# Score chunks of the first head inside the last context tiles, and an output projection in three parts

## The reference

```
x = x + cross_attention(layernorm(x), ctx)   # ctx: 4096 x 512
x = x + state_space(layernorm(x))
x = x + experts(layernorm(x))

cross_attention: q, k, v of x (16 heads, 4 kv heads of 128), k and v of ctx;
  q, k, k_ctx with a root-mean-square norm per head, q and k also rotated;
  keys = 4096 of ctx and 256 own ones (causal); softmax; @ wo
state_space: z, xBC, dt = u @ W_in; causal convolution of 4 taps and silu on xBC;
  dt = softplus(dt + bias); two chunks of 128 tokens: decays exp(cs_l - cs_s) under
  the diagonal, y = (C B^T * decays) (x dt) + C state + D x; y = y * silu(z);
  y = y * rsqrt(mean(y*y) + eps) * norm_weight; @ W_out
experts: top 6 of 32 experts (192 wide) by sigmoid scores, and a shared one (384 wide)
```

## Time and profile before

| | |
|---|---|
| time of the runs (3) | median 1052.37 us, 1051.82 to 1052.49 |
| the profiled execution | 1051.38 us |
| its span, first to last instruction | 1049.3 us |
| TensorE busy | 1035.7 us (99%) |
| VectorE busy | 777.2 us (74%) |
| ScalarE busy | 602.7 us (57%) |
| GpSimd busy | 182.4 us (17%) |
| granted TensorE clock | 1.00 over the whole span |

### The profile page before, as it was taken

The page is one execution under the profiler, slowest core; times in us unless marked ns, Lnnn a source line. Parts: engine busy times, 40 slices in busy tenths (PEclk is TensorE's granted clock), DMA queues, the critical chain, the costliest instruction groups (busy, mean ns, idle before and its releaser), DMA issues.

```text
span 1049.3 us, 15552 instructions
## 1 busy us (share of the span) xinstructions
PE 1035.7 (99%) x5789; PEld 885.7 (84%) x5789; DVE 777.2 (74%) x1661; ACT 602.7 (57%) x1090; POOL 182.4 (17%) x200
## 2 busy tenths in 40 slices
PE   7999999999999999999999999999999999999998
PEld 6888888887888888888888888888886888888887
DVE  5856777648777777777877777877668877777775
ACT  4344434334865566665566666568448466666664
POOL 4643344330000000000000000002202112222221
PEclk9999999999999999999999999999999999999999
DMA  6658675498004240042200431004450376555540
GB/s 235 233 195 286 229 241 173 133 317 293 37 1 139 73 131 1 1 171 81 91 1 1 171 121 56 1 1 182 161 231 1 121 285 214 195 191 183 190 169 21
DMA packets 64155, 145.76 MB, mean 139 GB/s; under 512 B 3888, under 2 KB 42704, under 8 KB 62672
## 3 DMA queue, kind: packets, MB, share of 16 engines
q1 hardware_dynamic: 64080, 144.77, 40.0%
HBM read 108.55 MB, written 36.21 MB: 138 GB/s over the span
## 4 chain that ended last, share of the span: by engine, by line
PE 95%; DVE 2%; ACT 1%; POOL 0%; issue 0%; DMA 0%; ACTq 0%
PE bank L549 18%; PE bank L486 16%; PE bank L592 12%; PE bank L569 11%; PE bank L467 11%; PE bank L847 8%; PE bank L594 6%; PE bank L849 4%; PE bank L649 2%; PE bank L662 1%; PE bank L496 1%; PE bank L780 1%; PE bank L717 1%; DVE e_hl L1192 0%; PE bank L818 0%; PE bank L521 0%
## 5 line engine op out<-in xcount | busy, mean ns | idle before, releaser
L1058 DVE TENSOR_TENSOR pT<-bank,pT 128x512 fp32r<-128x512 f32 x272 | 184.8, 689 | 103.3 <-ACT pT L1485 101.5
L1485 ACT CAST pT<-bank 128x512 fp32r<-128x512 f32 x272 | 156.1, 594 | 142.7 <-PE bank L569 139.5
L592 PE MATMUL bank<-pT,vN 128*128 128x512 f32 (+1 forms) x544 | 225.7, 422 | 0.0
L549 PE MATMUL bank<-kT,qT_hi 128*128 128x512 f32 (+2 forms) x576 | 214.5, 391 | 2.1 <-DVE scores L1002 2.1
L1002 DVE TENSOR_SCALAR_CACHE_REDUCE scores<-bank 128x512 f32<-128x512 f32 x256 | 172.8, 686 | 1.7
L569 PE MATMUL bank<-ident,scores 128*128 128x128 f32 x1072 | 161.3, 272 | 0.4 <-DVE pT L1058 0.3
L1456 ACT ACTIVATE scores<-scores,neg_max 128x1024 f32<-128x1024 f32 (+2 forms) x128 | 154.0, 1203 | 5.7 <-DVE neg_max L1014 5.7
L594 PE MATMUL bank<-pT,vN 128*128 128x256 f32 (+1 forms) x544 | 152.5, 280 | 0.0
L486 PE MATMUL bank<-w_ctx_hi,ctx_hl 128*128 128x512 f32 x512 | 146.0, 398 | 6.5 <-ACT ctx_hl L1365 6.5
L847 PE MATMUL bank<-fT_parts,e_hl 128*128 128x512 f32 x392 | 140.0, 395 | 0.1
L569 PEld LDWEIGHTS bank<-ident,scores 128*128 128x128 f32 x1072 | 127.2, 140 | 12.1 <-DVE pT L1058 1.2
(11 more groups left out here) (224 smaller groups left out, 1563.9 us busy)
## 6 DMA issues: line engine op xcount, KB each, us to landing
e_raw<-in_experts SPq DMA_DIRECT2D x51, 768.0 KB, 4.3
k_spill<-k_stage SPq DMA_DIRECT2D x16, 1024.0 KB, 4.5
v_spill<-v_stage SPq DMA_DIRECT2D x16, 1024.0 KB, 8.4
vN<-v_spill SPq DMA_DIRECT2D x16, 1024.0 KB, 5.2
kT<-k_spill SPq DMA_DIRECT2D x15, 1024.0 KB, 5.3
ctx_raw<-in_ctx SPq DMA_DIRECT2D x15, 512.0 KB, 4.3
w_raw<-in_w_qkv SPq DMA_DIRECT2D x6, 1024.0 KB, 5.0
wo_sb<-in_wo SPq DMA_DIRECT2D x4, 1024.0 KB, 9.5
```

The source lines that it names most:

```text
L549: done = e.matmul(bank[b][:, 0:n], qT[a][:, h, qt * P:(qt + 1) * P], kT[:, w, lo:lo + n], start=m == 0, stop=m == 2)
L592: e.matmul(halves[:, :, q0:L], vN[:, 0, kt, :], ring[:, :, i * L + q0:(i + 1) * L], start=kt == 0, stop=False)
L1058: e.tensor_tensor(ring[:, 1, :], bank[tb][:, :], ring[:, 0, :], ALU.subtract).then_inc(p_lo, 1)
L1485: e.copy(ring[:, 0, :], bank[tb][:, :]).then_inc(p_hi, 1)
```

## The change

**Chunks.** Nine early chunks of head 0 (all seven of qt 0, two of qt 1) are issued inside tiles 29, 30 and 31, one after each of the first three groups of `project(i)`, in banks 6 and 7 by turns; VectorE evicts them ahead of the rest of that tile. The five early chunks that are left use banks 0, 2, 6, 7, 0; three of them come ahead of `turn(NT - 1)`, two behind it. The third group starts again at bank 0. Four chunks of head 1 are made ahead, not eight. The regions v and s01 change places in the SBUF, and `chunk_max` moves to keep.

**Last tile.** ScalarE squares k of tile 31 ahead of the copy of tile 30's k. VectorE puts the low part of k of tile 30 in the place of the low part of v of tile 31, which it makes after both maxima of head 0. SP loads three pieces of v before it spills the last batch.

**Output projection.** w_out is loaded in two halves (the first with w_z, the second after wo), split by ScalarE (times norm_weight) and VectorE; y turned is split too (ScalarE copies, VectorE subtracts); `project_y` makes three products of each. Padding x waits for the first four splits. The load of expert tile 4 waits for the end of the projection.

**Decays.** For the second token tile ScalarE makes all eight heads of a half; PE's order of the decay turns and `y_rows(0, 0)` changes with it.

**Start of the experts.** The low parts of the first expert tiles are made in pieces between other steps, the first tokens are turned between the two column groups of the projection, the first logits come after the first gate products, and the second token tile's copies change places.

```diff
+EARLY = 3
-        for i, c in enumerate(EARLY_CHUNKS):
-            self.add(0, 0, c, (0, 2, 6, 7)[i % 4])
-        self.first = list(range(len(self.chunks)))
-        for c in EARLY_CHUNKS:
-            self.add(0, 1, c)
-        self.second = list(range(len(self.first), len(self.chunks)))
+        for i, (qt, c) in enumerate([(qt, c) for qt in range(2) for c in EARLY_CHUNKS]):
+            self.add(0, qt, c, (6, 7)[i % 2] if i < EARLY * 3 else (0, 2, 6, 7)[(i - EARLY * 3) % 4])
+        self.first = {NT - EARLY + i: list(range(3 * i, 3 * i + 3)) for i in range(EARLY)}
+        self.second = list(range(3 * EARLY, len(self.chunks)))
...
-        for _ in range(8):
+        for _ in range(4):
             self.ahead.append(self.add(1, *ahead.pop(0)))
...
-        sizes = dict(keep=12288, k=34816, v=34816, spare=16096, s01=34816, s23=34816, pt=12288, q=32768)
+        sizes = dict(keep=12288, k=34816, s01=34816, spare=16096, v=34816, s23=34816, pt=12288, q=32768)
...  (TensorE, project)
+                    if i in plan.first and k < KD - 1:
+                        in_turns([plan.first[i][k]], None)
...  (TensorE, after the tiles)
-            for s in plan.first:
-                in_turns([s], None)
+            in_turns(plan.second[:3], None)
             turn(NT - 1)
-            for s in plan.second + plan.third + plan.ahead:
+            for s in plan.second[3:] + plan.third + plan.ahead:
                 in_turns([s], None)
...  (TensorE, state space)
+            y_rows(0, 0, dsub_a, 1)
+            decay_rows(1, 0, 1, bnat_st, 2)
             decay_rows(1, 1, 0, xr, 6)
             decay_rows(1, 1, 1, gated_z, 4)
-            decay_rows(1, 0, 1, bnat_st, 2)
-            y_rows(0, 0, dsub_a, 1)
...  (TensorE, project_y)
+                pe.wait_ge(wo2_lo, 4 * half + 4)
...
-                        done = e.matmul(bank[b][:, 0:n], yT[:, k, tt * P:(tt + 1) * P], w_out[:, k, lo:lo + n], start=k == 0, stop=k == DI // P - 1)
+                        done = three(bank[b][:, 0:n], lambda a: yT[a][:, k, tt * P:(tt + 1) * P],
+                                     lambda w: w_out_lo[k][:, lo:lo + n] if w else w_out_hi[:, k, lo:lo + n], k == 0, k == DI // P - 1)
...  (TensorE, experts)
-            turn_rows(4, 0, fn)
-            project_y(1, 1)
-            route_logits(0)
+            project_y(1, 1, turn_between=turn_first_tokens)
...
             up_half(0, 0)
             up_half(1, 0, (0,))
+            route_logits(0)
...  (VectorE, one tile: after(i))
+                if i < NT - 1:
+                    rest_of_v(i)
+                else:
+                    rest_of_k(i - 1)
...  (VectorE, tiles)
+                if i in plan.first:
+                    for s in plan.first[i]:
+                        evict(s)
+                if 1 <= i < NT - 1:
+                    rest_of_k(i - 1)
+                after(i)
...  (VectorE, after the tiles)
+            for s in plan.second[:2]:
                 evict(s)
             rest_of_k(NT - 1)
+            for s in plan.second[2:]:
                 evict(s)
             for qt in range(2):
                 for s in plan.third[2 * qt:2 * qt + 2]:
                     evict(s)
                 maximum(0, qt)
+            rest_of_v(NT - 1)
             for s in plan.ahead:
                 evict(s)
...  (VectorE, splits)
+            def rest_of_w_out(k):
+                src = w_out_raw[k // 4][:, k % 4, :]
+                dve.wait_ge(wo2_hi, k + 1)
+                dve.wait_ge(pv, NH * NPAIR)
+                e.scalar_tensor_tensor(out=w_out_lo[k][:, :], in0=src, scalar=nw[:, k:k + 1], in1=w_out_hi[:, k, :],
+                                       op0=ALU.mult, op1=ALU.subtract).then_inc(wo2_lo, 1)
+            for k in range(4):
+                rest_of_w_out(k)
...
             mask_gram()
+            rest_of_w_out(4)
+            rest_of_w_out(5)
             mask_rows(0, 0)
+            rest_of_w_out(6)
             x_rows(1, 0)
-            decay_rows(1, 0)
+            rest_of_w_out(7)
             mask_rows(0, 1)
-            decay_rows(1, 1)
...  (ScalarE, tiles)
-                if i >= 1:
+                if 1 <= i < NT - 1:
                     main_of_k(i - 1)
-                after(i)
+                squares_of_k(i)
+                if i == NT - 1:
+                    main_of_k(i - 1)
+                main_of_v(i)
...  (ScalarE, splits and decays)
+            for k in range(6):
+                main_of_w_out(k)
...
+            def second_decay_rows(c, between=None):
+                act.wait_ge(wo2_lo, 6 + 2 * c)
+                for q in range(2):
+                    h0, b = 8 * c + 4 * q, BANK_DEC[1, c][q]
+                    act.wait_ge(drow, DROWS.index((1, c, q)) + 1)
+                    for i in range(4):
+                        done = e.activation(decays[1][:, h0 + i, :], bank[b][:, i * P:(i + 1) * P], ACT.Relu, bias=cs[:, 1, h0 + i:h0 + i + 1], scale=-1.0)
+                    done.then_inc(dsub_a, 1)
...
+                e.activation(rows, rows, ACT.Exp, scale=-1.0).then_inc(dec_e, 2)
...  (SP)
+            sp.wait_ge(ctx_proj, NT)
+            for p in (0, 1, 2):
+                wait_spilled(v_out, p)
+                load_v(0, p)
             spill(NBATCH - 1)
-            for p in (0, 1, 2, NPIECE - 1, NPIECE - 2):
+            for p in (NPIECE - 1, NPIECE - 2):
...
+            e.dma_start(w_out_raw[0][:, :, :], t["w_out"][:, 0:4]).then_inc(w_out_in[0], 16)
             sp.wait_ge(wo_done, TT)
-            e.dma_start(w_out[:, :, :], t["w_out"]).then_inc(w_out_in, 16)
+            e.dma_start(w_out_raw[1][:, :, :], t["w_out"][:, 4:8]).then_inc(w_out_in[1], 16)
...  (SP, load_e)
+                        sp.wait_ge(e_lo_first, 1)
+                    elif j == 4:
+                        sp.wait_ge(yp, 3)
```

More of the change, by code:

```diff
@@ L163, in before, with last_in @@
         return self.bank_history[bank][k - 1] if k else None
+    def last_in(self, bank):
+        return self.bank_history[bank][-1][1]
     def last_chunk(self, h):
@@ L275, in build_program @@
         pT = [reg.take(f"pT{i}", [2, 512], F32R) for i, reg in enumerate([region["pt"]] * 3 + [sp_])]
-        chunk_max = [sp_.take(f"chunk_max{i}", [NCHK]) for i in range(4)]
+        chunk_max = [keep.take(f"chunk_max{i}", [NCHK]) for i in range(4)]
         row_max = [sp_.take(f"row_max{i}", [1]) for i in range(4)]
@@ L522, in own_turn @@
                 done.then_inc(own_turned, 1)
-            for i in range(NT):
-                project(i)
-                if i == 1:
-                    pe.wait_ge(consts, 7)
-                    for tt in range(TT):
-                        pe.wait_ge(ln_out, tt + 1)
-                        turn_rows(tt, tt, xn)
-                if i >= 1:
-                    turn(i - 1)
-                n, half = step_of(i)
-                if 1 <= n <= NSTEP and half == 0:
-                    own_turn(n - 1)
-                if 0 <= n < NSTEP and half == 0:
-                    own_project(n)
             def score(s):
@@ L622, in spread_sums @@
                 done.then_inc(spread, 1)
-            for s in plan.first:
-                in_turns([s], None)
+            for i in range(NT):
+                project(i)
+                if i == 1:
+                    pe.wait_ge(consts, 7)
+                    for tt in range(TT):
+                        pe.wait_ge(ln_out, tt + 1)
+                        turn_rows(tt, tt, xn)
+                if i >= 1:
+                    turn(i - 1)
+                n, half = step_of(i)
+                if 1 <= n <= NSTEP and half == 0:
+                    own_turn(n - 1)
+                if 0 <= n < NSTEP and half == 0:
+                    own_project(n)
+            in_turns(plan.second[:3], None)
             turn(NT - 1)
-            for s in plan.second + plan.third + plan.ahead:
+            for s in plan.second[3:] + plan.third + plan.ahead:
                 in_turns([s], None)
@@ L1548, in act_program @@
             e.activation(ecs[:, :], cs[:, 1, :], ACT.Exp).then_inc(dec_exp, 1)
+            def second_decay_rows(c, between=None):
[6 more added lines that the diff above has]
+                    done.then_inc(dsub_a, 1)
+                    if q == 0 and between:
+                        between()
+                rows = decays[1][:, 8 * c:8 * c + 8, :]
+                act.wait_ge(dsub_a, 2 * c + 4)
+                e.activation(rows, rows, ACT.Exp, scale=-1.0).then_inc(dec_e, 2)
             def decay_rows(tt, c):
```

169 lines of the change are left out of this document (105 added, 64 removed).

## The result

The changed kernel takes 1055.11 us in the median of 8 runs (1054.44 to 1055.26), the kernel before 1052.32 in 8 runs beside it (1050.57 to 1052.62). The ratio is 1.0028, 95% interval 1.0019 to 1.0037: slower by 2.8 us. The profiled execution of the changed kernel took 1055.26 us with a span of 1053.4; that of before 1051.38 with 1049.3.

A forecast was written before the change was run, and what follows sets the result against it. TensorE, busy 99% of the span and 95% of the last chain, was taken to bound the kernel. Moved chunks +7.1 and output projection -2.3 gave +4.8 us on 1052.37: 1057.2 us, range 1051.5 to 1061.5.

The forecast's parts named there:

- Chunks inside the tiles cost nothing more: Tiles 29 to 31: nine moved chunks cost their own 5.83 us of TensorE work and add no waits.
- The last turn: End of the last tile: TensorE idle 1.3 us until it can turn the normalised keys at 240.27.
- The bank of the first late chunk: Late chunks of head 0: bank 0 waits for all 14 evictions, TensorE idle 2.3 us.
- The store of v and TensorE's wait: Head 0: late last v spill holds ScalarE's first pT copy, then VectorE, then TensorE, idle 5 us.
- The slow restart: Rival: after the 5 us wait twelve matmuls run at half clock, +2.4 us, 1059.6 us; chance 0.17.
- The crowded queue: Rival: the v spill meets the loads of v and k, takes 11.6 us: +4.0, 1061.2 us; chance 0.07.
- Sum of part 1: Move of nine chunks into the last three tiles, with its waits up to head 0's third step: +7.1 us.
- Part 2: Output projection in three products, with weight splits, decays and experts' start: -2.3 us, bounds -3.0 and 0.
- the wait for the first tokens: Last layer: the 0.5 us wait before the first tokens are turned goes, as they are turned between column groups.
- three places: Split of turned tokens, logits, second tokens: TensorE there before VectorE, waits of 0.1 to 0.3 us, summed as 0.35.
- From profile to median: Whole kernel: median of runs taken 0.99 us above the profiled 1051.38, giving base 1052.37 us.

The follow-up runs named there:

- the fills: Changed kernel with matmuls of no use in TensorE's two longest waits, two versions: 1053.19 us (ratio 1.0012) and 1053.28 us (1.0018).
- the three kernels of that experiment: Changed kernel with v's last low part earlier, with last spills ahead of the v loads, and with both: 1055.04, 1054.44, 1049.91 us.
- part 1 alone: Kernel before with the chunk and last-tile edits, without those of output projection, decays and experts' start: 1057.24 us, ratio 1.0052.
- the mended kernels: Kernels with the chunk and last-tile edits plus low part of v early, last spills first, late chunks from bank 1: 1048.81 us; without output-projection edits 1050.75.
- part 2 alone: Changed kernel with chunk and last-tile edits undone, output projection in three products kept: 1049.80 us, ratio 0.9981 to the kernel before.
- the mended part 1: Kernel before with chunk and last-tile edits, low part of v early, last spills first, late chunks from bank 1; no output-projection edits: 1050.75 us, ratio 0.9989.
- v early: Changed kernel with only the low part of v of the last tile earlier on VectorE: 1055.04 us, ratio 1.0033 to the kernel before.
- spills first: Changed kernel with only the last spills ahead of the three v loads on the DMA queue: 1054.44 us, ratio 1.0024 to the kernel before.
- both: Changed kernel with the low part of v earlier and the last spills ahead of the v loads: 1049.91 us, ratio 0.9983 to the kernel before.
- bank one first: Changed kernel with the late chunks beginning in bank 1 in place of bank 0: 1054.46 us, ratio 1.0027 to the kernel before.
- the shorter fills: Changed kernel with 8 and 10 matmuls of no use in TensorE's two waits, without the wait for the last keys' copy: 1053.28 us, ratio 1.0018.

## Why the prediction was right, and where its sizes were off

The forecast was slower, +4.8 us, 1057.2; measured were +2.8 and 1055.1. Direction and mechanism were right, several terms were not.

- *Chunks inside the tiles cost nothing more.* Right: the nine put the turn of tile 30 back by 5.97 us against the turn of tile 27; 5.83 was their price.
- *The last turn.* Forecast idle 1.3, measured 0.90.
- *The bank of the first late chunk.* Forecast 2.3, measured 2.17, of the same cause: it is released by the last early chunk's eviction.
- *The store of v and TensorE's wait.* The term that was most off. The idle was 5.0 in the forecast and 2.6 in the trace. Half of the difference is that TensorE itself came 1.2 us later, counted from the turn of tile 31 (260.00 - 244.87 = 15.1 in place of 13.9), delayed by its low clock: with the first wait filled it got there at 13.6 (259.95 - 246.34). The other half is the landing: TensorE goes on 17.7 us behind that turn in place of 18.9. The store was issued 1.4 us later than forecast (10.1 behind the turn for 8.8) and landed 1.3 sooner (15.7 for 16.9), so the transfer, which I had set to 8.2 us from issue, was 2.7 too long. Of these, 0.6 is a slip of reading: landings are counted from the start of the issue, and I added the 0.58 us of the issue to 7.6. The rest is the size itself, set by a least of 7.1. The landings of all sixteen stores of v in the changed kernel, and the last stores of k and v alone:

```profile
DMA to landing us min/median/max: 5.5/8.3/11.5
...
k_spill<-k_stage SPq DMA_DIRECT2D x1, 1024.0 KB, 10.8
v_spill<-v_stage SPq DMA_DIRECT2D x1, 1024.0 KB, 5.5
```

  The 5.5 is a new least. In the kernel before each store of v was issued directly behind a store of k, so its landing held that one's transfer too; here 8 us lie between the two issues (247.06 and 255.00), and the store of k, held up behind the three loads, lands at 257.8, 2.7 us ahead of that of v. The sixteen rows were a sample of another case, and their least was no bound for this one.
- *The slow restart.* It had a chance of 0.17 (though the text beside it says "about as likely as not"), "a wait of 5 us" as its condition and +2.4 us as its price. It is what happens, twice, behind waits of only 2.2 and 2.6 us; and the fills show that it costs what the second stretch loses, 1 to 2 us in the median. It should have been in the sum: that the time did not come out too low for want of it is in part luck, as the store of v landed 1.3 us sooner than forecast.
- *The crowded queue.* Its 11.6 us for the store did not come about in the changed kernel, but its mechanism did. I let the three loads pass for done since they had been issued 12 us before; the store of k that stood behind them landed 2.8 us after the store of v was issued (257.8 for 255.00). The store of v was so late that little of this delay showed in its own 5.5 us; when v was moved early the price came almost to the letter (11.4). The mistake was to see only the store of v behind the loads, and not the store of k ahead of it. The Trainium skill ("DMA: Bandwidth & Descriptors", Queues, rings and completion order) has descriptors consumed in ring order; the three kernels of that experiment agree with it (store of k: 10.9 us behind the three loads, 4.4 and 4.5 ahead of them).
- *Sum of part 1.* At the first turn of head 1 the kernel with part 1 alone is 6.9 us behind the kernel before; forecast +7.1. The agreement is in part luck: an earlier landing by 1.3 us against a low clock of about 1.7. At the end of the span it is 5.8, in the medians 5.5. So of the 1.6 us between 7.1 and 5.5, only 0.2 stood at the first turn of head 1; 1.1 came off in the later stages, by a pace that is not explained (below), and 0.3 between span and median. The forecast total was 2.0 too high: these 1.6, less 0.3 for part 2, and 0.7 by which the two parts measured alone add up to more than both together, which the intervals allow.
- *Part 2.* Forecast -2.3, measured -2.0. The threes come every 0.70 and 0.35 us, the wait for the first tokens is gone, the diagonal product waits 0.22 (forecast 0.35). The waits that I lumped at 0.35 for three places are mainly one of 0.67 at the down products.

```profile
814.17 0.63 PE L480 MATMUL bank<-w_out_hi,yT 128*128 128x512 f32 x2
...
814.87 0.63 PE L480 MATMUL bank<-w_out_hi,yT 128*128 128x512 f32 x2
...
824.79 0.40 PE L480 MATMUL bank<-w_out_hi,yT 128*128 128x256 f32 x2
825.03 0.28 PE L480 MATMUL bank<-w_out_lo,yT 128*128 128x256 f32 x1
825.14 0.40 PE L480 MATMUL bank<-w_out_hi,yT 128*128 128x256 f32 x2
```

(Those are of the changed kernel's projection, to be held against the earlier trace rows.)

- *From profile to median.* I set the forecast 0.99 above the sum made on the profile, as if the offset were the same for both kernels. It was not. The runs of before beside the experiments come in two kinds by their mean granted clock: 51 at 0.998 with a median of 1052.11 and 38 at 1.000 with 1051.56. The profiled execution was of the second kind. So before loses some clock in most of its runs too, and the difference of medians is some tenths smaller than that of the profiles. That it is lost behind the 2.1 us wait is likely, as the mended kernels, whose longest wait in this stretch is 1.3 us, had 1.000 in nearly all runs (11 of 11 and 8 of 9), and the kernel with part 2 alone, which keeps that wait, had it in 4 of 11; no trace shows such a run of before.

*What stays open.* Every kernel with part 1 runs a little faster than before where neither has a wait: 0.48 us less from the first turn of head 1 to that of head 15 and 0.65 us less over the expert tiles, the same to 0.05 us in four kernels, while the kernel with part 2 alone keeps to the pace of before within 0.01. It is no single step (none differs by over 0.03 us). It gives back 1.1 us of part 1's cost. Part 1 also exchanges two regions of the SBUF and shifts the instruction streams; which of these does it was not tried. For the mended part 1 this 1.1 us is nearly all of its gain of 1.2.

## What to carry to other kernels

When a load is moved ahead of a store in a queue, follow the store to whoever waits for its landing. Here two edits, the late operand and the crowded queue, each hid the other: undoing one alone gave nothing that the measurement could tell, both gave 5 us. Ask also what else stands in that queue between the load and the store. Price a wait on TensorE with the low clock that may follow it, and ask whether a later wait takes that loss (and any gain ahead of it) back. And before filling a wait with useful work, look at what that work puts ahead of the next engine's critical step.

## What the runs showed of the hardware

- The granted clock fell to the 1.2 GHz level behind waits of 2.17 to 4.5 us, in each of the six traces that have such waits (the changed kernel, part 1 alone, v early, spills first, both, bank one first); behind waits of 1.6 us and less it did so in no trace. Ahead of the waits of 2.5 us and more TensorE had worked without a pause for over 4 us; the one of 2.17 us always followed a wait of 0.9 us, with 1.7 us of work between them. Behind the 2.1 us wait of before it did not fall in the profiled execution, nor in that of part 2 alone. The loss differs between executions of one kernel (mean clock 0.995 to 0.998). The Trainium skill ("TensorE: Matmul & The Clock Gate", What's actually happening) says that idleness sends the clock down and activity brings it back; the traces agree in kind.
- Matmuls whose product nobody reads, put into such waits, kept the clock at 1.00 (11 of 11 and 8 of 11 runs, where the changed kernel had it in none of 8) and made the kernel 1 to 2 us faster. In the kernel with the shorter fills the three runs at 0.998 took 2.6 us more in the median (1055.54) than the eight at 1.000 (1052.96).
- A store of 1024 KB took 4.4 to 11.4 us from issue to landing, according to what stood ahead of it in its queue. Behind three loads and the store of k, the store of v landed 2.7 us after that of k, whether it was issued 2.2 or 7.9 us after it.
